# A routed expert layer on one core: each tile's results scattered to their tokens' rows, instead of gathered at the end

## The reference

```
logits = flat @ gate_W + gate_b                 # flat: 2048 tokens x 256, 8 experts
top_v, top_i = jax.lax.top_k(logits, 2)
w = jax.nn.softmax(top_v, axis=-1)
w_full = jnp.zeros((N, 8)).at[arange(N)[:, None], top_i].add(w)
for e in range(8):
    mid = gelu(flat @ exp_W1[e] + exp_b1[e])    # 256 -> 1024
    y_e = mid @ exp_W2[e] + exp_b2[e]           # 1024 -> 256
    out = out + w_full[:, e:e + 1] * y_e
x = x + out                                     # then layer norm
```

## Time and profile before

| what | us |
|---|---|
| median of 3 runs | 2791.5 (2788.26 to 2793.62) |
| the profiled execution, its own time | 2784.09 |
| its span, first to last instruction | 2782.3 |
| PE busy (its share of the span) | 2507.6 (90%) |
| DVE busy | 1495.4 (54%) |
| ACT busy | 1326.7 (48%) |
| POOL busy | 455.7 (16%) |
| mean granted TensorE clock | 0.957 of full speed |

### The profile page before, as it was taken

One profiled execution on the slowest core, in us unless ns is written; L12 is line 12 of the kernel. 1 busy time (PEld: TensorE's weight loads), 2 busy tenths in 40 slices (PEclk: granted clock), 3 DMA queues, 4 the chain that ended last, 5 costly groups with the idle time before them and its releaser, 6 DMA issues. The chain is left out here.

```text
span 2782.3 us, 47352 instructions
## 1 busy us (share of the span) xinstructions
PE 2507.6 (90%) x15751; PEld 1434.3 (52%) x15752; DVE 1495.4 (54%) x4204; ACT 1326.7 (48%) x2826; POOL 455.7 (16%) x735
## 2 busy tenths in 40 slices
PE   6999999999979889999699999999998988599991
PEld 3555544444444456676355544444445555367661
DVE  2555777888644500013455688878756664322224
ACT  2655466677754521211355556666675544122220
POOL 4233212101100000000113312122121122120004
PEclk8999999999999999999799999999999988699995
DMA  7555534232800022203654452332422454111103
GB/s 224 159 142 142 144 92 110 54 80 62 260 1 1 1 97 89 72 12 137 189 141 142 135 131 67 84 103 62 109 67 90 138 159 161 67 63 32 34 30 97
DMA packets 156895, 276.78 MB, mean 99 GB/s; under 512 B 22928, under 2 KB 98960, under 8 KB 152208
## 3 DMA queue, kind: packets, MB, share of 16 engines
q1 hardware_dynamic: 152896, 262.56, 33.0%
q0 software_dynamic: 3792, 11.54, 1.3%
HBM read 195.51 MB, written 95.29 MB: 105 GB/s over the span
## 5 line engine op out<-in xcount | busy, mean ns | idle before, releaser
L1634 ACT ACTIVATE second_p<-psum 128x512 f32<-128x512 f32 (+3 forms) x1024 | 462.1, 521 | 264.6 <-PE psum L1435 251.9
L1634 ACT ACTIVATE first_p<-psum 128x512 f32<-128x512 f32 (+3 forms) x768 | 366.7, 548 | 163.7 <-PE psum L1435 160.4
L1732 DVE TENSOR_REDUCE second_max_parts<-psum 128x1 f32<-128x512 f32 x512 | 322.7, 684 | 68.7 <-PE psum L1412 64.8
L1732 DVE TENSOR_REDUCE first_max_parts<-psum 128x1 f32<-128x512 f32 x512 | 322.9, 684 | 61.7 <-PE psum L1412 59.2
L1728 DVE CUSTOM_DVE_ANT_0 second_masked<-psum,mask_qk 128x384 f32<-128x384 f32 (+3 forms) x512 | 229.7, 489 | 192.7 <-PE psum L1412 163.4
L1447 PE MATMUL psum<-second_p,second_v_aug 128*32 128x512 f32 (+3 forms) x2048 | 235.5, 532 | 5.5 <-ACT second_p L1634 4.8
L1425 PE MATMUL psum<-second_q,second_k 64*128 64x512 f32 (+3 forms) x1024 | 225.4, 436 | 6.9 <-DVE second_max_parts L1728 4.5
L1412 PE MATMUL psum<-second_k,second_q 64*128 64x512 f32 (+3 forms) x1024 | 199.8, 387 | 30.4 <-DMA second_k<-a_k_parts 13.6
L1435 PE MATMUL psum<-second_shift_T,choose 64*128 64x512 f32 (+3 forms) x1024 | 197.6, 381 | 0.0
L1425 PEld LDWEIGHTS psum<-second_q,second_k 64*128 64x128 f32 x1024 | 97.8, 186 | 189.5 <-ACT second_p L1634 81.0
L2511 ACT ACTIVATE routed_space<-psum,routed_bias 128x128 f32<-128x128 f32 x312 | 84.9, 383 | 214.5 <-PE psum L2436 214.5
(11 more groups left out here) (341 smaller groups left out, 3865.4 us busy)
## 6 DMA issues: line engine op xcount, KB each, us to landing
first_k<-c_k_parts SPq DMA_DIRECT2D x64, 256.0 KB, 4.7
second_q<-a_q_parts SPq DMA_DIRECT2D x128, 128.0 KB, 3.0
second_k<-a_k_parts SPq DMA_DIRECT2D x128, 128.0 KB, 3.0
second_k<-c_k_parts SPq DMA_DIRECT2D x64, 256.0 KB, 4.8
first_q<-a_q_parts SPq DMA_DIRECT2D x64, 128.0 KB, 3.2
first_k<-a_k_parts SPq DMA_DIRECT2D x64, 128.0 KB, 3.1
c_k_parts<-first_held SPq DMA_DIRECT2D x16, 512.0 KB, 3.1
first_q<-c_q_parts SPq DMA_DIRECT2D x64, 128.0 KB, 4.3
```

The costliest lines, as they stand in the source:

```text
L1634: evacuated(act.activation(probs[tile % 2][:, 2 * h + p, q0:SEQ], bank[:, q0:SEQ], ACT.Exp, scale=scale), event)
L1732: evacuated(v.reduce_max(max_parts[n % 2][:, h, p, qt, k0 // BANK:k0 // BANK + 1], bank[:, 0:width], axis=AX_X), event)
```

## The change

The last stage no longer gathers. `expert_results` is now laid out by token: row x*2048 + token holds the result of the token's expert number x (`home`), followed by 128 rows that nobody reads (`2 * T + n`). A second table in DRAM, `row_home` (16384 numbers of 4 bytes), says for each region row where its result belongs. It is filled once with the numbers of the unread rows, at the end of `first`; each of the 32 sends gets a second indirect transfer that writes 128 numbers of 4 bytes. Those of batches 0 to 2 are issued in `second`, right behind each batch's row sends; batch 3's eight are POOL's first work in `routed`. In `routed` SP loads a tile's 128 home rows (512 bytes) beside its rows, and POOL scatters the tile's results by them; a scatter waits until the scatter before it has landed. POOL's 16 additions of the residual move into the last five steps, between scatters. The last stage loads 4 MB in 8 plain transfers from SP, two for each chunk. DVE's eight instructions for `result_at` go. The core of the diff:

```diff
 # stage_between
+                if front and front[0] == "shares":
+                    for n in range(CHUNKS):
+                        for x in range(2):
+                            at = x * T + n * SEQ
+                            sp.dma_start(gathered[:, n * QT:(n + 1) * QT, x, :],
+                                         results_dram[at:at + SEQ, :].rearrange("(q p) d -> p q d", p=P)).then_inc(got[n], 16)
...
-                if front and front[0] == "gather":
-                    for t in range(NT):
-                        for x in range(2):
-                            pool.indirect_dma_start(gathered[:, t, x, :], None, results_dram[:, :],
-                                                    bass.IndirectOffsetOnAxis(ap=place[:, x, t:t + 1], axis=0)
-                                                    ).then_inc(got[t], 16)
...
-                                    v.wait_ge(got[t], 32)
+                                    v.wait_ge(got[n], 32)
 # stage_attentions
                     for dst, src, done in fills:
                         sp.dma_start(dst, src).then_inc(done, 16)
+                if home_fill:
+                    dst, done = home_fill
+                    sp.wait_ge(astray_made, 1)
+                    sp.dma_start(dst, astray[:, :]).then_inc(done, 16)
...
+                    pool.iota(home[:, :, :], [[T, 2], [P, NT]], base=0, channel_multiplier=1).then_inc(gate_numbers, 1)
...
                     if b == BATCH - 1:
                         pool.wait_ge(gate_sent, 16 * 2 * NT)
+                        pool.wait_ge(home_sent, 16 * 2 * (NT - QT))
+                        return
+                    for t in range(b * QT, (b + 1) * QT):
+                        for x in range(2):
+                            pool.indirect_dma_start(gate["home_dram"][:, :], bass.IndirectOffsetOnAxis(ap=place[:, x, t:t + 1], axis=0),
+                                                    home[:, x, t:t + 1], None).then_inc(home_sent, 16)
 # stage_routed_experts, SP
-                    if done := tile_at(s, pair, 3):
-                        t, r, _ = done
-                        sp.wait_ge(y_read, t + 1)
-                        sp.dma_start(results_dram[bass.ds(t * P, P), :], result[r][:, :]).then_inc(stored[r], 16)
+                    if at := tile_at(s, pair, 2):
+                        t, r, before = at
+                        wait_for(sp, stored[r], before * 16)
+                        sp.dma_start(home[r][:, :], home_dram[bass.ds(rows_of(sp, t), P), :]).then_inc(home_in[r], 16)
...
+                for s in range(2):
+                    body(s, 0)
+                sp.wait_ge(home_sent, 16 * 2 * QT)
 # stage_routed_experts, POOL
+                        pool.wait_ge(home_sent, 16 * 2 * QT)
+                        pool.wait_ge(home_in[r], (before + 1) * 16)
+                        pool.wait_ge(y_read, t + 1)
+                        wait_for(pool, stored[1 - r], (before + r) * 16)
+                        pool.indirect_dma_start(results_dram[:, :], bass.IndirectOffsetOnAxis(ap=home[r][:, :], axis=0),
+                                                result[r][:, :], None).then_inc(stored[r], 16)
...
+                for t in range(NT - QT, NT):
+                    for x in range(2):
+                        pool.indirect_dma_start(home_dram[:, :], bass.IndirectOffsetOnAxis(ap=gate["place"][:, x, t:t + 1], axis=0),
+                                                gate["home"][:, x, t:t + 1], None).then_inc(home_sent, 16)
```

More of the change, by code:

```diff
@@ L349, in stage_between @@
         HELD = 4 if front and front[0] == "combine" else 8
-        if front and front[0] == "gather":
-            _, share, place, results_dram = front
+        if front and front[0] == "shares":
+            _, share, results_dram = front
             gathered = sb("gathered", [P, NT, 2, D])
-            got = [sem(f"got{t}") for t in range(NT)]
+            got = [sem(f"got{n}") for n in range(CHUNKS)]
         if normed:
@@ L2350, in stage_routed_experts @@
         down_bias = sb("down_bias", [P, EXPERTS, D])
+        home = [sb(f"home{i}", [P, 1], U32) for i in range(2)]
+        home_sent, home_in = sem("home_sent"), [sem(f"home_in{i}") for i in range(2)]
         residual_in, down_bias_in, twice = sem("residual_in"), sem("down_bias_in"), sem("twice")
```

68 lines of the change are left out of this document (42 added, 26 removed).

## The result

| | us |
|---|---|
| kernel before, median of 4 runs beside the change | 2790.4 (2788.26 to 2793.62) |
| changed kernel, median of 4 runs | 2820.8 (2819.01 to 2824.75) |
| ratio | 1.011, 95% interval 1.0092 to 1.0128 |
| profiled execution of the change, own time and span | 2824.75, 2822.9 |

What follows compares the result with a forecast made beforehand. It took POOL's issuing of gathers to bound the last stage and PE's products the routed stage. Terms -15.6 + 2.0 - 1.3 - 1.3 = -16.2 us from the median 2791.5 gave 2775, range 2770 to 2784.

Steps and rivals of the forecast that it cites:

- The last stage: Last stage: plain loads replace gathers bound by POOL's issuing, DVE becomes the bound, 38.8 us instead of 54.4, 15.6 less.
- C: Last stage: the eight loads share the engines evenly, first chunk lands with the last, 8.5 us more, 2784; chance 0.08.
- D: Last stage: the loads are no faster than the gathers, 2791, no change; chance 0.04.
- tile 6's rows: Routed stage: these rows are asked for before the residual, so PE's wait goes, 1.3 us less (0 to 2).
- rival B: Routed stage: the scatter chain becomes the pace; each us over 7.8 costs 38, 2813 at 8.8; chance 0.02.
- The handover: End of routed: the last scatter lands at 2728.6 instead of the store's 2726.6, 2.0 us more (1.1 to 3.8).
- The start of routed: Start of routed: PE starts 2.8 us earlier, but tile 3's rows wait for eight number sends; 1.3 less in all.
- lands 3.7 later at 2412.7: Start of routed: landing of the last of eight number sends, started at 2409.0, for which SP waits before tile 3's rows.
- Cost 0, covered by PE's own work: `second`: eight more sends a batch, 10.1 us, delay the augment within its slack of 11.9 and 15.5 us, costing nothing.
- at batch 2 POOL has nothing to do: `second`, third batch: POOL is idle until batch 3's places come, so that batch's number sends cost 0.
- Rival A: Number sends of 4 bytes to 128 scattered places cost more than row sends; 2797 at twice the price; chance 0.05.
- from c = 1.49: Price in us of one number send above which Rival A decides; the gain is used up at 2.3.

Runs made afterwards that it cites:

- run 15: The version of run 14 with the last wait for the scatters' landing on SP instead of POOL: ratio 0.9942 against the kernel before; repeated, 0.9953.
- run 14: The changed kernel without number sends, the number carried in the row (258 wide), DVE making the home row: 2775.6 against 2788.5 of before, ratio 0.996.
- run 2: The kernel before with only the 24 number sends of `second` added, which nobody reads: 2807.3 against 2772.8, ratio 1.0138.
- the repeat of the sends alone: The kernel before plus the 24 unread number sends of `second`, as in run 2, measured again on another chip: 2824.5 against 2790.2, ratio 1.0124.
- run 11: The kernel before plus the 24 unread number sends, with one wait for the row sends' landing ahead of each batch's number sends: 2811.8 against 2790.2, ratio 1.0079.
- run 1: The changed kernel without the 24 number sends of `second`, the results table filled ahead: 2777.1 against 2772.8 of before, ratio 1.0017.
- run 6: The changed kernel with each batch's eight number sends in `second` behind POOL's next augment (third batch: behind the last row sends): 2833.3, ratio 1.0166 to before.
- run 13: The kernel before plus 24 sends of whole 1 KB rows to an unread table, with an added DVE wait: 2817.8 against 2790.2, ratio 1.0097.
- run 3: The changed kernel with the 24 number sends of `second` replaced by 1 KB row sends to a spare table, plus a DVE wait: 2799.9, ratio 1.0098 to before.
- run 12: The kernel before plus the 24 unread number sends, these and the first three batches' row sends in pairs, each waited for: 2893.1 against 2790.2, ratio 1.0362.

## Why the prediction was wrong

- **The last stage: right.** Forecast -15.6, measured -15.7. DVE began 6.4 us after the first load's issue (6.1 forecast), the chunks stood 7.1 apart (7.2), without gaps, and the loads came in order. Rivals C and D did not come.
- **Routed: right.** Forecast -1.3 for tile 6's rows. Measured -1.1: in before profiled again the third step between results takes 8.8 us, in the change 7.9, where PE has no pause now (294.7 to 294.9 in all ten profiles with scatters, 296.0 to 297.4 in the ten with stores). DVE never waited for `stored`: rival B did not come.
- **The handover: right mechanism, wrong size.** Forecast +2.0 with bounds 1.1 and 3.8; measured +4.8, and +5.5 counted to ACT's first instruction, from which the prediction counts (it stands 0.7 us ahead of the first gather in before, beside the first load now; the last stage is then 16.5 shorter). I had put a landing of 3.7 in place of 1.7. The rows show that POOL issues the last scatter 0.9 us after the result's end (the store: at once), that scatters land in 2.4 to 4.3, and that the next stage's first load comes 7.7 us after the scatter's issue, 5.3 more than the landing. Before needs 2.0 from its store's landing to the next transfer; of the other 3.3, run 15 shows 1.6 to go when SP waits in POOL's place, and the rest stays open. My upper bound took the boundary's cost as equal for a stage that SP ends and one that POOL ends.
- **The start of routed: the failed step is "lands 3.7 later at 2412.7".** The first half was right: the rows came early, PE turned tile 0 2.2 us after the load's issue, not 5.1. But number sends land 6.3 to 11.4 us after their issue, held up the rows of tile 1 and, through SP's wait, tile 3's. Forecast -1.3, measured +10.1. The profiles of the version of run 14, without them, have 33.4 to 35.2 us, as before.
- **`second`: the failed step is "Cost 0, covered by PE's own work".** I priced a send right (0.96 and 0.30), found the one instruction behind it on POOL, and compared 10.1 us with a slack of 11.9. In the change's own profile the augment was harmless; but the 11.9 held a stand of PE's at the row of eight, and on chips A, which have no such stand, the slack was too short: PE waited 5.3 and 4.4 us for the augment (run 2). There the mechanism of the prediction came, with the slack mis-sized. On chips B what I left out is that sends hold up PE without any wait in the program. The trace of before had it: PE stood 4.0 and 3.3 us at the first two rows of eight, with a releaser that the profile could not name. I read there only whether PE waited at the augment's product. And "at batch 2 POOL has nothing to do" left out DVE's wait for the landing of that batch's row sends, which came 9.0 us after the last one's issue in run 2, against 2.4 at the first two batches. In the change the cost is +35.4, of it some 27.5 PE idle and 7.9 PE at the lower clock (119.4 us busy against 111.5 in before profiled again, for the same 925 instructions).
- **Rival A had the right culprit and the wrong coin.** It asked what 4 bytes to 128 places would cost, but in issue time on POOL, decided "from c = 1.49", and gave itself 0.05. The issue time of a number send was 0.96 throughout. The rule that I weighed there, the Trainium skill, "SBUF — State Buffer", section Who interferes with whom, has DVE stopping GpSimd; these traces show POOL's sends never delayed, and PE, then ACT and DVE behind it, the ones that stand. The same section of the Trainium skill says that a DMA never contends with a compute engine. The repeat of the sends alone (beside run 11), where PE stands 16.6 us at batch 0's sends without waiting for them or for the augment, sits ill with that; whether the transfers do it, or POOL's writing of them, no run shows.
- **The chances** summed mechanisms that I could write down as a wait. Nothing stood for an effect of 24 more transfers on the neighbours, with 0.07 for everything slower.

**What stays open** is why PE is late. Against a backlog in the queue, which I believed in for a while: paced row sends land 1.8 to 2.0 us after their issue, and a quarter of the rows costs two thirds. For a limit on how long POOL may issue without a pause: the stand begins at the seventh or eighth send, and a gap of 1.7 us resets it. Against it: the second stand comes when POOL issues nothing, and chips A have no first one at sixteen sends. Against a lack of instructions: the two instruction queues of the change's trace move nothing between 2251 and 2290, and the engines go on in between. The traces with stands are also thinner where they matter (17 of DVE's 104 semaphore updates are missing around the change's sends, none in run 1), so the lateness of a single signal is surer than their number. I did not try gaps by other POOL work of a known length; the 0.9 us of an augment reset nothing to speak of in run 6. What sets chips A and B apart here, and whether it is the chip at all, no run shows.

## What to carry to other kernels

Price a transfer issued from POOL three times: its issue on POOL against the slack of what waits behind it, what it does to the engines beside it in a long row, and how long it takes to land; here only the first was in the sum, with a slack read from one profile. A slack that contains a stand shrinks where the stand is missing, so take it from more than one profile. A small fact that belongs to a row should travel in the row: 8 bytes behind 1 KB cost nothing measurable, and the same fact sent alone cost 34 us in one stage and 10 in the next. And where a trace shows waits "remote" or "issue" around the very operation that a change doubles, that is a price, if only a lower bound: read it before the slack, and look up which engine raises the semaphore.

## What the runs showed of the hardware that was not expected

- On chips B a row of 16 indirect transfers issued by POOL without a pause held PE up, and ACT and DVE behind it, for 12 to 17 us (the change, the repeat of the sends alone, run 13), with 4 bytes and with 1 KB a row; after a pause of 1.7 us they worked beside the next six (run 11). On a chip A rows of 16 held nothing up (runs 2 and 3). The 24 sends cost 34.5 us on the one and 34.3 on the other, by different waits.
- Eight scatters of 128 x 4 bytes to DRAM left the transfer engines with a share of 0.7 to 1.2 at 34 to 44 GB/s for some 12 us (the repeat of the sends alone); a pair of them makes POOL wait 7.0 us, a pair of 128 x 1 KB 2.5 us (run 12). A 1 MB load issued behind them in the change took 21.4 us, where the median of its kind is 6.7. The Trainium skill, "DMA: Bandwidth & Descriptors", section Latency and other measured facts, has tiny transfers at a floor of about 0.8 us; the wait for a pair of these, with 128 scattered targets each, lies at about nine times that.
- A plain store waited for by SP lets the next stage start 3.7 us after the result; with scatters it takes 5.7 where SP waits for them and 7.3 where POOL does (runs 14 and 15), 8.6 in the change.
